# One change to an attention and feed-forward kernel: chunk 4's feed-forward moved between slots, and the end of the program in another order

## The reference

```python
x = _layernorm(x + attention(x, w_qkv, w_out, b_out, w_th))   # 16 heads of 64
x = _layernorm(x + ffn(x, w_up, w_down))                      # 128 -> 512 -> 128
```

```python
x_norm = x / (rms(x) + 1e-8);  y = einsum('bsd,fd->bsf', x_norm, ternary(w))
```

## Time and profile before

| | |
|---|---|
| median of 3 runs | 239.44 us (239.44 to 240.01) |
| profiled execution | 239.48 us, its span 237.7 us |
| TensorE busy | 221.2 us, 93% of the span |
| VectorE busy | 177.2 us, 75% |
| ScalarE busy | 168.0 us, 71% |
| GpSimd busy | 100.3 us, 42% |
| granted TensorE clock, mean | 0.981 |

### The profile page before, as it was taken

How to read it: one execution, slowest core, us unless ns; L and a number is a source line. 1 busy time by engine, 2 the same in 40 slices (tenths; PEclk the granted TensorE clock), 3 DMA queues, 4 the chain that set the end, 5 groups by cost and what they waited for, 6 DMA issues and landing times.

```text
span 237.7 us, 9733 instructions
## 1 busy us (share of the span) xinstructions
PE 221.2 (93%) x4200; PEld 203.5 (86%) x4200; DVE 177.2 (75%) x459; ACT 168.0 (71%) x313; POOL 100.3 (42%) x118
## 2 busy tenths in 40 slices
PE   7999989999999999999999999999999969989880
PEld 7899879888999898999989898989898959978770
DVE  0675799987877975688767966896679787884954
ACT  2686557676666669866997599768986787575671
POOL 7035204513151415761666265724574367212232
PEclk9999999999999999999999999999999988999995
DMA  6947570020002000200021002100101001000002
GB/s 209 286 106 196 174 172 7 3 66 3 3 13 58 26 3 12 59 25 4 11 61 38 14 3 69 40 11 3 57 17 42 3 4 43 26 4 22 3 3 66
DMA packets 19106, 11.67 MB, mean 49 GB/s; under 512 B 2232, under 2 KB 18168, under 8 KB 18936
## 3 DMA queue, kind: packets, MB, share of 16 engines
q1 hardware_dynamic: 18324, 10.47, 15.7%
q10 hardware_dynamic: 740, 0.59, 0.8%
HBM read 8.91 MB, written 2.10 MB: 46 GB/s over the span
## 4 chain that ended last, share of the span: by engine, by line
PE 52%; DVE 14%; issue 14%; ACT 10%; POOL 9%; POOLq 0%; DVEq 0%; ACTq 0%
PE bank L1103 8%; PE bank L1105 7%; PE bank L1104 7%; PE bank L1252 7%; PE bank L1226 6%; PE bank L1210 4%; DVE CTl L879 4%; POOL xw L506 3%; POOL E L519 2%; ACT CTh L584 2%; POOL rstd L549 2%; PE bank L1184 2%; PE bank L1158 2%; ACT y L707 1%; DVE mx L891 1%
## 5 line engine op out<-in xcount | busy, mean ns | idle before, releaser
L519 POOL TENSOR_TENSOR E<-E,rc 128x400 f32<-128x400 f32 x32 | 27.9, 872 | 80.3 <-DVE rc L901 80.3
L879 DVE TENSOR_TENSOR CTl<-bank,CTh 128x512 fp32r<-128x512 f32 x64 | 41.2, 686 | 27.6 <-ACT CTh L584 27.6
L584 ACT ACTIVATE Yb<-bank 128x512 f32<-128x512 f32 x64 | 38.5, 602 | 27.9 <-PE bank L1105 26.7
L584 ACT ACTIVATE CTh<-bank 128x512 fp32r<-128x512 f32 x64 | 34.8, 600 | 8.7 <-PE bank L1252 8.6
L1103 PE MATMUL bank<-xTh,Gh 128*128 128x256 f32 x128 | 39.0, 305 | 0.3 <-DVE Gl L828 0.2
L1103 PE MATMUL bank<-CTh,Mh 128*128 128x256 f32 x128 | 37.1, 290 | 0.5 <-DVE CTl L879 0.5
L1104 PE MATMUL bank<-CTl,Mh 128*128 128x256 f32 x128 | 36.4, 284 | 0.0
L1105 PE MATMUL bank<-CTh,Ml 128*128 128x256 f32 x128 | 36.3, 284 | 0.0
L1104 PE MATMUL bank<-xTl,Gh 128*128 128x256 f32 x128 | 35.8, 280 | 0.0
L1105 PE MATMUL bank<-xTh,Gl 128*128 128x256 f32 x128 | 35.7, 279 | 0.0
L1252 PE MATMUL bank<-AT,xw 50*128 50x256 f32 x384 | 31.1, 294 | 3.3 <-DVE AT L884 3.3
(11 more groups left out here) (143 smaller groups left out, 476.3 us busy)
## 6 DMA issues: line engine op xcount, KB each, us to landing
raw<-in_L_attn_x SPq DMA_DIRECT2D x37, 64.0 KB
pt_rows<-PT SPq DMA_DIRECT2D x2, 512.0 KB, 5.0
R<-pt_rows SPq DMA_DIRECT2D x1, 1024.0 KB, 5.1
xr<-in_L_attn_x SPq DMA_DIRECT2D x6, 128.0 KB
out<-y SPq DMA_DIRECT2D x6, 128.0 KB, 1.9
raw<-in_L_attn_x SPq DMA_DIRECT2D x13, 56.0 KB
w_sb<-in_L_attn_w_qkv SPq DMA_DIRECT2D x2, 256.0 KB, 4.9
w_sb<-in_L_attn_w_qkv ACTq DMA_DIRECT2D x2, 256.0 KB, 4.9
```

The lines of the kernel that those rows point to most:

```text
L519: tt(e, e, rc[s % 2][:, :].unsqueeze(2).broadcast_to([P, TILES, WIN]), ALU.mult).then_inc(s_norm, 1)
L584: copy = lambda o, i, **k: nc.scalar.activation(o, i, ACT.Copy, **k)
L879: v.tensor_tensor(ct_view(CTl[s // 4 % 2], s % 4, q), c_view(s, q), ct_view(f32(CTh[s // 4 % 2][:, :, :]), s % 4, q), ALU.subtract).then_i ...
```

## The change

- ffn(s): chunk 4 has step -1 in slot 25, steps 0 and 1 in slot 26, 2 in 27, and so on to 6 in slot 31. Before, step k was in slot 26 + k.
- In slot 26 residual(4) stands ahead of total, variance_roots(4) ahead of normalise, input_scale(4) and up_input(4) behind total. second_sum(3) goes ahead of total(27); second_sum(4) enters slot 30 from the tail.
- All chunks up to 4: x1_T and x1_hi go from step 1's slot to step 2's (x1_T behind the transposes, x1_hi ahead of y_out(s, 0)); x1_lo goes behind shift(s); up behind the O part, for chunk 4 behind queries(s, 1). gelu(4) stands behind y_out(27, 1).
- second_sum computes weight and hden ahead of its wait for down_back.
- The tail: hidden_low(6) goes from VectorE to GpSimd; the first hidden_high(7) from ScalarE to VectorE; down(6) behind up(7), down_back(6) behind down(7); the order of results, shifts and norms and the number of dummy matmuls change.

```diff
--- before.py
+++ after.py
@@ -290,7 +290,10 @@
 
         def ffn(s):
 
-            return [(n, s - first) for n, first in enumerate(FIRST) if -1 <= s - first < (9, 9, 9, 9, 6, 1)[n]]
+            steps = [(n, s - first) for n, first in enumerate(FIRST) if n != 4 and -1 <= s - first < 9]
+            if s >= FIRST[4] - 1:
+                steps += [(4, k) for k in {25: [-1], 26: [0, 1]}.get(s, [s - 25])]
+            return [(n, k) for n, k in steps if n < 5 or k < 1]
 
         UP_BANK = {5: (1, 0), 6: (2, 0), 7: (6, 5)}
         AT_BANK = {7: 5}
@@ -528,7 +531,9 @@
             def hidden_low(n, t):
 
                 pool.wait_ge(f_gh, 2 * n + t + 1)
-                need(pool, f_dn, n)
+                need(pool, f_dn, 0 if n == 6 else n)
+                if n == 6:
+                    pool.wait_ge(f_gl, 12 + t)
                 o = slice(2 * t, 2 * t + 2)
                 tt(gTl[gset(n)][:, o, :], gT[gset(n)][:, o, :], f32(gTh[gset(n)][:, o, :]), ALU.subtract).then_inc(f_gl, 1)
 
@@ -556,11 +561,13 @@
                         fold_squares(n)
                     if k == 5:
                         hidden_root(n)
+                    if k == 0 and n == 4:
+                        variance_roots(n)
                 normalise(s)
                 for n, k in ffn(s):
-                    if k == 0:
+                    if k == 0 and n != 4:
                         variance_roots(n)
-                    if k == 6:
+                    if k == 6 and n < 4:
                         last_root(n)
                 if s == 1:
                     rows_high(1)
@@ -573,8 +580,10 @@
             variance_roots(6)
             variance_roots(7)
             hidden_root(5)
+            hidden_low(6, 0)
+            hidden_low(6, 1)
+            last_root(5)
             hidden_root(6)
-            last_root(5)
             hidden_root(7)
             last_root(6)
             last_root(7)
@@ -647,15 +656,20 @@
                     copy(Y_out(b, part // 8 % 2, 2 * (part % 8)),
                          bank[y_bank(s, b)][:, :].rearrange("p (h t i) -> p h t i", h=2, i=IL)).then_inc(s_Ye, 1)
 
+            add_bias = lambda o, i: nc.scalar.activation(o, i, ACT.Identity, bias=b_sb[:, 0:1])
+
+            def first_column(n):
+
+                need(act, f_aT, n)
+                add_bias(attnS[:, CHUNK - 1:CHUNK], bosT[:, n // 4:n // 4 + 1])
+
             def stage(n):
 
                 need(act, f_aT, n)
-                add_bias = lambda o, i: nc.scalar.activation(o, i, ACT.Identity, bias=b_sb[:, 0:1])
                 if n % 4 < 3:
                     act.wait_ge(s_O, n + 1)
                     add_bias(attnS[:, :], bank[O_BANK][:, 0:CHUNK]).then_inc(f_stage, 1)
                 else:
-                    add_bias(attnS[:, CHUNK - 1:CHUNK], bosT[:, n // 4:n // 4 + 1])
                     act.wait_ge(s_O, n + 1)
                     add_bias(attnS[:, 0:CHUNK - 1], bank[O_BANK][:, 0:CHUNK - 1]).then_inc(f_stage, 1)
 
@@ -723,6 +737,9 @@
                 if s >= TURN:
                     ct_hi(s - 2)
                     at_hi(s - 1)
+                for n, k in ffn(s):
+                    if k == 2:
+                        x1_hi(n)
                 if s > TURN:
                     y_out(s, 0)
                 if s < TURN:
@@ -735,21 +752,25 @@
                 act.wait_ge(s_sub, s + 1)
                 nc.scalar.activation(e, e, ACT.Exp).then_inc(s_exp, 1)
                 for n, k in ffn(s):
-                    if k == 2:
+                    if k == 2 and n < 4:
                         gelu(n, 0)
                         gelu(n, 1)
                 if s >= TURN:
                     y_out(s, 1)
+                for n, k in ffn(s):
+                    if k == 2 and n == 4:
+                        gelu(n, 0)
+                        gelu(n, 1)
                 if s < len(IN_STEP):
                     fills(IN_STEP[s])
                 for n, k in ffn(s):
                     if k == -1:
+                        if n % 4 == 3:
+                            first_column(n)
                         stage(n)
                 for n, k in ffn(s):
                     if k == 4:
                         down_out(n)
-                    if k == 1:
-                        x1_hi(n)
                     if k == 3:
                         hidden_high(n, 0)
                         hidden_high(n, 1)
@@ -765,8 +786,9 @@
             gelu(5, 1)
             hidden_high(5, 0)
             hidden_high(5, 1)
+            result(4)
             x1_hi(6)
-            result(4)
+            first_column(7)
             squares(5, 0)
             stage(7)
             squares(5, 1)
@@ -778,11 +800,11 @@
             squares(6, 0)
             squares(6, 1)
             x1_hi(7)
+            gelu(7, 0)
+            gelu(7, 1)
+            act.wait_ge(f_gh, 15)
+            hidden_high(7, 1)
             down_out(6)
-            gelu(7, 0)
-            hidden_high(7, 0)
-            gelu(7, 1)
-            hidden_high(7, 1)
             squares(7, 0)
             squares(7, 1)
             down_out(7)
@@ -941,12 +963,15 @@
 
             def hidden_high(n, t):
                 dve.wait_ge(f_gelu, 2 * n + t + 1)
-                need(dve, f_dn, n)
+                dve.wait_ge(f_gh, 2 * n + t)
+                need(dve, f_dn, {7: 5}.get(n, n))
                 o = slice(2 * t, 2 * t + 2)
                 v.tensor_copy(gTh[gset(n)][:, o, :], gT[gset(n)][:, o, :]).then_inc(f_gh, 1)
 
             def hidden_low(n, t):
                 dve.wait_ge(f_gh, 2 * n + t + 1)
+                if n == 7:
+                    dve.wait_ge(f_gl, 14 + t)
                 need(dve, f_dn, {5: 0, 6: 0, 7: 5}.get(n, n))
                 o = slice(2 * t, 2 * t + 2)
                 v.tensor_tensor(gTl[gset(n)][:, o, :], gT[gset(n)][:, o, :], f32(gTh[gset(n)][:, o, :]), ALU.subtract).then_inc(f_gl, 1)
@@ -959,12 +984,12 @@
             def second_sum(n):
 
                 dve.wait_ge(f_hroot, n + 1)
-                dve.wait_ge(f_back, n + 1)
                 dve.wait_ge(f_ratio, n + 1)
                 v.scalar_tensor_tensor(out=weight[:, :], in0=hroot[:, :], scalar=EPS_RMS, in1=ratio[:, n % 4, :],
                                        op0=ALU.add, op1=ALU.mult).then_inc(f_weight, 1)
                 v.tensor_scalar(hden[:, :], hroot[:, :], EPS_RMS, None, ALU.add).then_inc(f_hden, 1)
                 dve.wait_ge(f_weight, n + 1)
+                dve.wait_ge(f_back, n + 1)
                 need(dve, f_store[own(n)], stored(n) - 16 * row_parts(n))
                 for i in range(CT):
                     v.scalar_tensor_tensor(out=y2[own(n)][:, i:i + 1, :], in0=x1n[own(n)][:, i:i + 1, :],
@@ -1003,9 +1028,6 @@
 
             dve.wait_ge(s_eps, 1)
             for s in range(STEPS):
-                for n, k in ffn(s):
-                    if k == 2:
-                        x1_lo(n)
                 if s == LAG + 1:
                     dve.wait_ge(s_pt, 32)
                 if LAG < s <= TURN:
@@ -1015,6 +1037,9 @@
                 if s > TURN:
                     ct_lo(s - 2)
                 shift(s)
+                for n, k in ffn(s):
+                    if k == 2:
+                        x1_lo(n)
                 if s == TURN:
                     ct_lo(s - 2)
                 for n, k in ffn(s):
@@ -1024,9 +1049,13 @@
                 if s >= TURN:
                     at_lo(s - 1)
                 for n, k in ffn(s):
-                    if k == 1:
+                    if k == 1 and n < 4:
                         input_scale(n)
                         up_input(n)
+                    if k == 0 and n == 4:
+                        residual(n)
+                    if k == 5 and n == 3:
+                        second_sum(n)
                 if s < 2:
                     absolute_sum(s)
                 if s == 2:
@@ -1037,8 +1066,11 @@
                     fills(IN_STEP[s - 1][-1:])
                 total(s)
                 for n, k in ffn(s):
-                    if k == 5 and n < 4:
+                    if k == 5 and n != 3:
                         second_sum(n)
+                    if k == 1 and n == 4:
+                        input_scale(n)
+                        up_input(n)
                     if k == 7:
                         result_shift(n)
                 if s < 2:
@@ -1063,19 +1095,16 @@
             ct_lo(30)
             at_lo(31)
             x1_lo(5)
-            second_sum(4)
+            second_norm(4)
             ct_lo(31)
-            second_norm(4)
             residual(6)
             result_shift(4)
-            hidden_low(5, 0)
             input_scale(6)
             up_input(6)
+            hidden_low(5, 0)
             hidden_low(5, 1)
             x1_lo(6)
             residual(7)
-            hidden_low(6, 0)
-            hidden_low(6, 1)
             hidden_sum(5)
             input_scale(7)
             up_input(7)
@@ -1083,6 +1112,7 @@
             x1_lo(7)
             second_norm(5)
             hidden_sum(6)
```

(22 more changed lines are left out.)

## The result

| | before | after |
|---|---|---|
| median | 239.62 us (4 runs, 239.44 to 240.01) | 243.78 us (4 runs, 242.86 to 244.81) |
| ratio | | 1.0172, interval 1.0126 to 1.0219 |
| profiled execution | 239.48, span 237.7 | 243.36, span 241.5 |
| mean granted clock | 0.981 | 0.980 |

The change makes the kernel slower by 1.7% (1.3 to 2.2), 4.2 us. The forecast was 242.3, in the range 238.4 to 244.4. Ratios leave out an execution more than 1.5% above the fastest of its kernel, which here is the profiled one of e2 alone (the median of e2 is 240.60 with it and 240.22 without it).

A forecast was written before the change was run, and what follows sets the result against it. TensorE's matmuls bound slots up to 27, chains through other engines the rest. Span 237.7 - 1.2 + 1.4 + 0.9 - 1.3 = 237.5; with 1.2 + 0.4 + 1.4 = 240.5; plus 1.8: 242.3 us, range 238.4 to 244.4.

The forecast's parts named there:

- Slots 11 to 26: Waits at x1_T and on AT go, but transposes then wait on normalise: -1.2 us, bounds -2.4 and -0.3.
- Slots 26 to 28: Chunk 4's earlier chain makes up(4) wait 0.8 for y2, and c_part(27) starts 1.4 us later.
- The port pair: GpSimd work holds up VectorE: +1.2 us at x1n(4), bounds 0 and 1.55; +1.4 in the tail from hidden_low(6).
- Slot 29: GpSimd's queue from normalise(28) through rows_low(7) to hidden_low(4) takes 5.5 us; TensorE stalls 2.4 before down(4).
- The sign that the fold would follow without a gap: In slot 29 the changed trace would show rows_low(7), hidden_low(4) and the fold without a gap on GpSimd.
- The sign that no x1_T would wait: The changed trace would show no wait of x1_T on TensorE.
- The clock: The low-clock stretch moves onto c_part(28), scores(30) and the transposes: 0 to +0.8 us, taken as +0.4.
- The tail without the port pair: From c_part(30) on, reordering and moved work gain 1.3 us, before any cost of hidden_low(6) on GpSimd.
- The port pair never bites: Rival, chance 0.20: GpSimd does not hold up VectorE; time 239.3 to 240.1 us, no change.
- The pile in slot 29 is absorbed: Rival, chance 0.20: rows_low(7) runs before normalise's chain needs GpSimd; time 237.1 us, or 238.4 halfway.
- A low-clock stretch in the tail: Rival, chance 0.05: a second one, 48 O matmuls at half pace, +1.3 us and more, 244 and above.

The follow-up runs named there:

- e2: The changed kernel with rows_low(7) on GpSimd moved from the end of slot 28 to the end of slot 27: 240.60 us, 1.004 of the kernel before.
- e4: The kernel before with only x1_T, x1_hi, x1_lo and up moved, chunk 4 keeping its slots: 237.11 us, 0.990 of the kernel before.
- e3: The changed kernel with hidden_low(6) back on VectorE: 241.86 us, 1.010 of the kernel before.
- e7: The changed kernel with chunk 4 in its old slots and hidden_low(6) back on VectorE: 235.14 us, 0.981 of the kernel before.
- e10: The changed kernel with hidden_low(6) still on GpSimd but waiting until second_sum(5) has written y2: 241.81 us, 1.011 of the kernel before.
- e9: The kernel before with 16 dummy matmuls ahead of c_part(28), in the stall of slot 30: 238.40 us, 0.995 of the kernel before.
- e1: The changed kernel with 16 dummy matmuls ahead of down(4), in the stall of slot 29: 242.38 us, 1.015 of the kernel before.
- e5: The changed kernel with chunk 4's chain back in its old slots: 237.41 us, 0.990 of the kernel before.
- e8: The changed kernel with rows_high(7) and rows_low(7) at the end of slot 27 and hidden_low(6) on VectorE: 237.90 us, 0.995 of the kernel before.

## Why the prediction was right

**Slots 11 to 26.** Forecast -1.2, measured -1.09 in the changed kernel (-1.2 less the 0.12 by which its loop begins late) and -1.2 in e4. That normalise would take over both removed waits was the reason for not writing 2.4: it ends six waits of TensorE in these slots now, 1.4 us.

**Slots 26 to 28.** y2(3) was to hold up(4) for 0.8; it was 1.07. c_part(27) came +1.31 for +1.4.

**The port pair.** The 1.2 us in slot 26 were 0.66 on input_scale, which normalise held, and 0.45 on x1n, which the copy held: 1.1. The 1.2 was a choice between the bounds 0 and 1.55, so that it came so near is in part luck. In the tail the forecast took one cut of 1.4 between x1n(7) and y2(5). There was one cut in x1n(7), 0.96, and a second in floor(5), 0.5, of which x1_lo(7) felt 0.4 (ScalarE had x1_hi(7) at 228.77, x1_lo(7) began at 229.14). e3, e7 and e10 show the cause. The rule of the Trainium skill (SBUF — State Buffer, section SBUF: two separate sides) is borne out by the rows above as far as the order goes: who starts first holds the pair. It is not the whole. In the kernel before a power of 1.01 us on 128x4 numbers started first, and two full-size subtractions with both inputs in SBUF ran beside it in 1.33 (1.29 with nothing beside them, e7):

```profile
221.22 1.01 POOL L525 TENSOR_TENSOR roots<-var_in,exps 128x4 f32<-128x4 f32 x1 [5.83 <-DVE var_in L918]
221.23 1.33 DVE L952 TENSOR_TENSOR gTl<-gT,gTh 128x512 fp32r<-128x512 f32 x2
```

The x1n(7) of the earlier trace rows ran in its 0.60 beside such a power too. And between the two halves of hidden_low(6) VectorE got in.

**Slot 29.** The pile on GpSimd was 5.5 us from normalise(28) to the end of hidden_low(4) in the rows of before; in after it was 5.6 (190.42 to 196.01). The wait of down(4) was forecast at 2.4 and was 2.26. e2 shows that this queue, not the table loads, sets slot 30. The sign that the fold would follow without a gap was wrong (0.80 idle), but the sum had the squares ahead of the fold in it and is untouched. The sign that no x1_T would wait failed too: x1_T(4) waits 0.44 and x1_T(7) 0.95, each for the x1n that GpSimd's work stretched.

**The clock, the term that was mis-sized.** The step reads "0 to +0.8 behind VectorE's slack. I take +0.4". The runs put 1.3 to 1.4 in its place: 1.3 between slot 30 and c_part(30) in e9 for before, 1.4 at c_part(30) and at the end in e1 for after, less the 0.3 by which e1 was already ahead at slot 29. Two things were wrong in it. The low stretch was 6 us long, where the forecast had only that of before, some 3. And the slack was thought to be VectorE's, but shift(30) waits for scores(30) and the transposes for TensorE, so that TensorE at half pace is itself the chain there. The missing 1.0 is the whole difference between the forecast span of 240.5 and the 241.5 measured; the other 0.4 up to the median of 243.78 is that the profiled execution (243.36) was the second fastest of four.

**The tail without the port pair.** Forecast -1.3; e3's tail is 1.26 shorter than before's (31.34 for 32.60). That is in part luck: the forecast took hidden_low(6) off VectorE, and in e3 it is back on it. With it on GpSimd but later (e10) the tail is 0.7 shorter than before's.

**The rivals.** "The port pair never bites" fell by the rows above. "The pile in slot 29 is absorbed" fell by the 2.26, and its mechanism was right: when rows_low(7) runs earlier (e2), 3.2 us come back, clock included. A low-clock stretch in the tail, while TensorE had work, came in the profiled executions of e2, e5 and e8, not in that of after.

## What to carry to other kernels

When a step moves one slot earlier, write out every queue that it enters there, the elementwise engine's above all: here one 2.4 us GpSimd instruction that had been harmless for six chunks stood ahead of the moved step and cost 3 us, some 1.4 of them by the clock behind the stall. Look at each GpSimd instruction of full size that will now run beside VectorE work of the kind that was stretched here, and mend it by time (a later start, idle room of the slot before) as well as by place. And where TensorE stands as long as the 2.0 and 2.3 us here, add what the clock may take behind it, on the path; a few matmuls into a free bank settle whether it does. Do it for the kernel before as well: it may have paid the same already, as this one had.

## What was not expected of the hardware

- The same stall of 2.26 us before down(4) was followed by a low-clock stretch of 6 us in the profiled execution of after, of about 3 in that of e3 and of none in that of e10. Stalls of 0.8 to 1.1 (e4, e5, e7) were followed by none in these slots, but in the tail of e5 stalls of 0.69 and 0.95, 2.3 us apart, were followed by one of about 3.5 us; after has nearly the same two there (0.68 and 0.95) and none behind them. In e1, e2, e8 and e10 TensorE waits 0.63 at c_part(30) and 0.78 at the transposes behind it, and in e2 and e8 alone some 3 us at half clock follow (207.5 to 210.5 in e8, busy all of it). This is likely why the changed kernel's runs are 2.0 us apart and those of e5 0.9; what decides it in one execution stays open.
- A VectorE copy of 128x512 from SBUF to the matmul type took 0.43 us (L969 in after). A copy of that size from PSUM, to plain f32, took 0.68 (L845), and the copy from SBUF with GpSimd's subtraction beside it 1.02 (e10).
- A VectorE instruction on 256 numbers took 0.81 us: it lasted until the GpSimd instruction beside it had ended.
